# A normed attention stage in a four-block image transformer: the turning of Q and K two passes behind the projection

## What is computed

```python
h = _L0_tok_ref(x, ...)
h = h + _L0_attn_ref(_layernorm(h), ...)
h = h + _L0_ffn_ref(_layernorm(h), ...)
h = h + _L1_attn_ref(_layernorm(h), ...)
h = h + _L1_ffn_ref(_layernorm(h), ...)     # the stage l1f
h = h + _L2_attn_ref(_layernorm(h), ...)
...
```

## Time and profile before

| | |
|---|---|
| median of three runs | 762.44 us (762.32 to 763.35) |
| profiled execution | 763.16 us, its span 761.4 us |
| PE, matmul | 708.0 us busy, 93% of the span |
| PE, weight load | 626.6 us, 82% |
| DVE | 494.7 us, 65% |
| ACT | 345.8 us, 45% |
| POOL | 164.4 us, 22% |
| chain that ended last | PE 68%, DVE 20%, issue 4%, POOL 3%, ACT 3%, DMA 1% |
| mean granted clock of TensorE | 0.946 of full speed |

### The profile page before, as it was taken

One profiled execution on the slowest core, in us unless ns is written; L12 is line 12 of the kernel. 1 busy time (PEld: TensorE's weight loads), 2 busy tenths in 40 slices (PEclk: granted clock), 3 DMA queues, 4 the chain that ended last, 5 costly groups with the idle time before them and its releaser, 6 DMA issues.

```text
span 761.4 us, 15938 instructions
## 1 busy us (share of the span) xinstructions
PE 708.0 (93%) x6222; PEld 626.6 (82%) x6222; DVE 494.7 (65%) x1231; ACT 345.8 (45%) x800; POOL 164.4 (22%) x164
## 2 busy tenths in 40 slices
PE   7799999999998799899899998999999999999996
PEld 6588898999985666688776787889999867789996
DVE  1748478888777836466553674478666768456784
ACT  0257354555452133576423432355544545247653
POOL 1200036444242021334111000016443220000000
PEclk9899999999999879899799997999999999769998
DMA  9912022223220000000200010032130200112100
GB/s 263 251 55 79 2 56 77 77 77 104 94 64 0 1 0 2 2 2 1 96 1 1 2 43 2 1 100 58 58 114 23 86 1 3 50 38 74 36 22 24
DMA packets 16200, 38.81 MB, mean 51 GB/s; under 512 B 3577, under 2 KB 4569, under 8 KB 15740
## 3 DMA queue, kind: packets, MB, share of 16 engines
q1 hardware_dynamic: 14150, 36.71, 16.6%
q10 hardware_dynamic: 1976, 1.08, 0.6%
HBM read 37.32 MB, written 0.44 MB: 50 GB/s over the span
## 4 chain that ended last, share of the span: by engine, by line
PE 68%; DVE 20%; issue 4%; POOL 3%; ACT 3%; DMA 1%; POOLq 0%; ACTq 0%; DVEq 0%; SPq 0%
PE PS L711 7%; PE PS L767 5%; PE PS L543 4%; PE PS L547 4%; PE PS L545 4%; PE PS L544 4%; PE PS L546 4%; PE PS L659 4%; PE PS L700 3%; PE PS L595 3%; PE PS L732 2%; POOL ssq L1767 2%; DVE AL L1438 2%; PE PS L596 2%; PE PS L597 2%
## 5 line engine op out<-in xcount | busy, mean ns | idle before, releaser
L936 ACT ACTIVATE MIX<-PS 128x288 f32<-128x288 f32 x118 | 48.5, 411 | 114.8 <-PE PS L547 114.6
L543 PE MATMUL PS<-XH,WH 128*128 128x288 f32 x284 | 87.3, 307 | 2.2 <-DVE OT L1427 1.4
L545 PE MATMUL PS<-XH,WL 128*128 128x288 f32 x284 | 84.7, 298 | 0.0
L544 PE MATMUL PS<-XL,WH 128*128 128x288 f32 x284 | 84.7, 298 | 0.0
L546 PE MATMUL PS<-X,WH 128*128 128x288 f32 x284 | 84.6, 298 | 0.0
L547 PE MATMUL PS<-X,WL 128*128 128x288 f32 x284 | 84.5, 298 | 0.0
L1740 POOL TENSOR_TENSOR rstd<-var,nhalf 96x3 f32<-96x3 f32 x18 | 15.3, 849 | 305.5 <-DVE var L1195 305.5
L1427 DVE TENSOR_TENSOR OT<-MIX,PS 128x288 f32<-128x288 f32 x94 | 42.3, 451 | 39.7 <-ACT MIX L936 39.0
L1438 DVE TENSOR_TENSOR AL<-OT,AH 128x288 fp32r<-128x288 f32 x118 | 59.0, 508 | 3.3 <-ACT AH L950 2.3
L1281 DVE TENSOR_TENSOR WL<-RG,WH 128x768 fp32r<-128x768 f32 (+2 forms) x46 | 57.9, 1258 | 4.4 <-ACT WH L916 4.3
L595 PE MATMUL PS<-AH,DW 128*128 128x288 f32 x166 | 52.6, 317 | 7.2 <-DVE AL L1438 7.0
(11 more groups left out here) (234 smaller groups left out, 1687.8 us busy)
## 6 DMA issues: line engine op xcount, KB each, us to landing
RG<-in_gu_l0f_dram SPq DMA_DIRECT2D x8, 512.0 KB, 4.6
RG<-in_gu_l0f_dram SPq DMA_DIRECT2D x16, 256.0 KB, 5.7
RG<-in_gu_l2f_dram SPq DMA_DIRECT2D x9, 384.0 KB, 3.5
RG<-in_gu_l2f_dram SPq DMA_DIRECT2D x18, 192.0 KB, 4.3
RD<-in_wd_l0f_dram SPq DMA_DIRECT2D x8, 384.0 KB, 3.2
RD<-in_wd_l2f_dram SPq DMA_DIRECT2D x9, 288.0 KB, 2.8
RD<-in_wd_l3f_dram SPq DMA_DIRECT2D x6, 384.0 KB, 3.2
BIG<-in_patch_dram SPq DMA_DIRECT2D x6, 288.0 KB, 7.5
```

The lines of the kernel that those rows point to most:

```text
L543: mm(o, WH[r][:, 0, w], XH[:, cols], start=True, stop=False)
L544: mm(o, WH[r][:, 0, w], XL[:, cols], start=False, stop=False)
L545: mm(o, WL[r][:, 0, w], XH[:, cols], start=False, stop=False)
```

## The change

The turning of unit u moves from pass u+1 to pass u+2 (`lag` = 2 for this stage alone), and with it the scores, the softmax, the turned probabilities and the product with V of each unit move one pass later, on PE, ACT and DVE. The loops have 18 passes in place of 17. `first_out` stays at pass 13, since the maximum of line 69 gives 13 for either lag, and so do the three parts of the next layer norm on DVE. `TX` gets a third buffer, and ACT's copy into it waits for the turning of unit u-3 in place of u-2. DVE's product with the power for unit i-1 runs at the head of pass i, ahead of `mean_square(i)`, in place of unit i's behind `shift` in pass i. No instruction is added or removed.

```diff
-        self.lag = 1 if token_major else 0
+        self.lag = 2 if qk_norm else 1 if token_major else 0
+        self.txs = 3 if qk_norm else 2
...
-            TX = [sb1(f"TX{r}", [TP, TAU * 256]) for r in range(2)]
+            TX = [sb1(f"TX{r}", [TP, TAU * 256]) for r in range(3)]
...
-                                          TX[u % 2][:, (2 * tau + k) * a.fq:(2 * tau + k + 1) * a.fq],
+                                          TX[u % a.txs][:, (2 * tau + k) * a.fq:(2 * tau + k + 1) * a.fq],
...
-                    act.wait_ge(S["qk_ready"], u0 + u - 1)
-                    activation(TX[u % 2][:, :], PSF[0:TP, 1024:1024 + TAU * 256], ACT.Copy).then_inc(S["tm_taken"], 1)
-
-                lag = 1 if a.tm else 0
+                    act.wait_ge(S["qk_ready"], u0 + u - 2)
+                    activation(TX[u % a.txs][:, :], PSF[0:TP, 1024:1024 + TAU * 256], ACT.Copy).then_inc(S["tm_taken"], 1)
+
+                lag = a.lag
...
-                    tx = TX[u % 2][:, 0:TAU * 2 * a.fq].rearrange("p (h d) -> p h d", d=64)
+                    tx = TX[u % a.txs][:, 0:TAU * 2 * a.fq].rearrange("p (h d) -> p h d", d=64)
...
-                lag = 1 if a.tm else 0
+                lag = a.lag
                 for i in range(a.units + lag + 4):
+                    if a.qk_norm and 1 <= i <= a.units:
+                        normalised_heads(i - 1)
                     if a.qk_norm and i < a.units:
                         mean_square(i)
...
                         shift(i - lag - 1)
-                    if a.qk_norm and i < a.units:
-                        normalised_heads(i)
```

More of the change, by code:

```diff
@@ L680, in qk @@
                                     last = mm(PS[VW * r:VW * (r + 1), k, tau * TP // 2:(tau + 1) * TP // 2].rearrange("f (i m) -> f i m", m=NB),
-                                              TX[u % 2][:, o:o + VW],
+                                              TX[u % a.txs][:, o:o + VW],
                                               cst[0:TP, 0:TP].rearrange("p (i r m) -> p r i m", r=2, m=NB)[:, r],
@@ L1252, in rotate @@
                 link(V.tensor_tensor(t2[:, 1:f2:2], src[:, 0:f2:2], si[:, 1:f2:2], ALU.mult))
-                V.tensor_tensor(TX[u % 2][:, 0:2 * TAU * VW].rearrange("p (n x) -> p n x", x=VW)[:, :, 0:a.fq],
+                V.tensor_tensor(TX[u % a.txs][:, 0:2 * TAU * VW].rearrange("p (n x) -> p n x", x=VW)[:, :, 0:a.fq],
                                 T2[:, f2:2 * f2].rearrange("p (n x) -> p n x", x=a.fq),
```

## The result

Before and after were run in turn on one chip: 762.58 us before (762.32 to 763.35, four runs), 752.76 us after (752.39, 752.75, 752.78 and 764.68). The ratio is 0.9868, with a 95% interval from 0.9849 to 0.9887. The forecast was 756.6 us and the range 752.0 to 761.3.

What follows compares the result with a forecast made beforehand. PE, busy 93% of the span, was taken as the bound, its passes paced by a 5.68 us DVE and POOL loop. Gains 2.4 + 3.1 + 0.3 = 5.8 us took 762.44 to 756.6 us; range 752 to 761.3.

Steps and rivals of the forecast that it cites:

- start, to the projection of pass 6: Stage start: lost time falls from 6.6 to 4.0 us, with a new 2.0 us wait for ACT's copy; 2.4 us taken.
- middle, to the end of pass 11: Passes 6 to 11: DVE's loop with POOL opens, passes fall from 5.68 to PE's 5.15 us; 3.1 us gained.
- end, to `l2a`: Stage end: lost time falls from 7.8 to 7.5 us, with new waits for `norm` of 1.5 and 2.5 us; 0.3 gained.
- the walk: Start gain counted by walking the times to the projection of pass 5, with 1.9 us of work moved behind: 2.2 us.
- The rival without half clock: No half clock after the new waits at start and end: 1.6 + 2.5 us more gain, 752.5 us; chance 0.14.
- passes over 5.2 us: Sign of being wrong: passes 6 to 11 longer than 5.2 us, where 5.15 was forecast.
- The rival of unchanged passes: Middle passes stay at 5.68 us, as the power stretches or something replaces the product: 759.7 us; chance 0.12.
- The step that `norm` would wait for the power's end: Middle: `norm`'s products wait for POOL's power, as a 1.22 us DVE operation took 1.83 beside POOL; loop 4.9 us, not 4.3.
- the rival of half clock through the stage's end: Half clock from pass 13 to the stage's end: 12.8 us more, 769.4 us; chance 0.06.
- one longer stretch: One 13.3 us half-clock stretch at the end costs 6.6 us, not 2.5: 760.7 us; chance 0.10, shared with no net effect.
- half clock already under the 36 records: Sign of being wrong: granted clock of 0.50 already during the 36 matmul records of the output projection, L767.
- Later stages keep their work: Behind the changed stage: later stages keep their work and their loads, which start earlier; no gain counted there.

Runs made afterwards that it cites:

- a3: The changed kernel as it is, run again on the third chip: 754.2 us, ratio 0.9890 to the kernel before.
- a2: The changed kernel as it is, run again on the second chip: 764.7 us, ratio 1.0017 to the kernel before.
- e1: The changed kernel with the product back behind `shift` in its own pass, so lag and third buffer only: 767.0 us, ratio 1.0044.
- e7: The changed kernel with the first half's output one pass later and six unread 288-column matmuls in each of passes 12 and 13: 753.0 us, ratio 0.9896.
- e8: The changed kernel, output where it was, with six unread 288-column matmuls in each of passes 12 and 13: 756.8 us, ratio 0.9928.
- e9: e7 with 14 more unread matmuls in pass 3, ahead of the projection that waits for ACT: 752.6 us, ratio 0.9899.
- b1: The kernel before with unread 288-column matmuls added, 24 in pass 2, 22 in pass 12, 6 in pass 13: 756.5 us, ratio 0.9904.
- e4: The changed kernel with the first half's output and the next layer norm's DVE parts one pass later: 753.9 us, ratio 0.9868.
- p3: The changed kernel with 22 unread 288-column matmuls between the changed stage and the next: 761.1 us, ratio 0.9983.

## Why the prediction was right, point by point

The total lay in the range, 3.8 us below the forecast, and the mechanism of the middle is the one forecast; that the total lay there is in part luck (below). The stage is cut here at the projection of pass 6 and at the end of pass 11, and the 2.5 us of work that the lag moves from the start to the end are set off. The gains on before, for all three profiles of the changed kernel:

| gain, us | forecast | after | a3 | a2 |
|---|---|---|---|---|
| start, to the projection of pass 6 | 2.4 | 2.1 | 0.6 | -1.6 |
| middle, to the end of pass 11 | 3.1 | 2.8 | 2.8 | 2.8 |
| end, to `l2a` | 0.3 | 1.3 | -3.3 | -5.5 |
| stage | 5.8 | 6.3 | 0.1 | -4.2 |

Only the middle came in every profile. The points that follow are of the first one, after.

**Start.** From the first projection to that of pass 6: 59.1 us before, 54.5 after; less 2.5 of moved work, a gain of 2.1 (forecast 2.4, or 2.2 by the walk). Each of its details came: the product at 302.17 behind `gates`, the transposes of unit 0 waiting 0.59 us (forecast 0.35), then

```profile
304.99 0.80 ACT L1097 ACTIVATE TX<-PS 96x768 f32<-96x768 f32 x1
...
305.84 4.57 PE L660 MATMUL PS<-wqkv_l1f,XT 128*96 128x256 f32 x12 [1.95 <-ACT TX L1097]
```

the wait for ACT's copy, and half clock over the projection behind it, 4.57 us as against the 4.63 of the earlier trace rows. The rival without half clock fell here, and again at 377.68.

**Middle.** From the projection of pass 6 to the end of pass 11: 34.1 us before, 31.3 after: 2.8 us for the forecast's 3.1. The pass is PE's own work, 5.20 us and not the 5.15 read from pass 5. That stands at the edge of the sign given for being wrong, "passes over 5.2 us" (they are 5.18 to 5.21 apart), but no other engine stands in the chain, so the 0.05 us is the size of PE's work. The rival of unchanged passes fell; e1 shows what it would have looked like.

**The shared ports.** The step that `norm` would wait for the power's end didn't come. In the fence of pass 8 above, L1620 and L1625, which both read SBUF twice, start 1.39 and 1.59 us into the 2.26 us power and end before it, in 0.16 and 0.46 us. In e1 the same two start at 357.02 and 357.22, between two powers, and take 0.16 and 0.46 us. The power took 2.26 to 2.27 us with `norm` beside it and without. So the reading of the earlier trace rows was carried to a pair to which it doesn't apply. The exclusive lock of the Trainium skill, SBUF — State Buffer, section "SBUF: two separate sides", which I had set beside it, isn't seen here: the trace disagrees for this pair. The loop from one sum of squares to the end of the product was 4.5 us by that (the product starts 0.03 us after the power ends, and DVE is idle for 0.72 of the pass's 5.21 us ahead of the next sum of squares) and not 4.9. Nothing in the sum hung on it.

**End.** From the end of pass 11 to `l2a`: 26.1 us before, 27.3 after, 2.5 of it moved work: a gain of 1.3 us for a forecast of 0.3. Of the difference 0.5 was a slip: the loss of before was counted from the end of pass 11, and pass 11's own 0.5 us, which had no part in it, was taken off again. The rest are sizes. Passes 12 and 13 lost 0.77 us and not 1.0, and for another cause, a wait that the forecast put at nothing: with no projection in front, pass 12's transposes come before ACT has taken the queries of unit 9 out of PSUM; the product of unit 11 and `shift(9)` were in time. And PE came to `l2a` 15.2 us after the 36 records, not 15.5.

**The clock in passes 12 and 13.** This is the step that failed, though not in the runs first timed. I counted passes 12 and 13 at full speed, with 1.0 us of waits, and gave the rival of half clock through the stage's end 0.06, and one longer stretch 0.10, because each wait was shorter than before. In two of the three profiled executions of the changed kernel half clock began there, with one wait of 0.77 us and small matmuls only, and in e1 it began behind none over 0.3 us. So waits shorter than those of before were no ground for full clock. That the first executions kept full clock there was luck: the sign given for being wrong, half clock already under the 36 records, came in a2 and a3. In the profiles with the fill, e7, e8 and e9, it never did. How the small difference at pass 3 becomes a longer half clock there and another in pass 12 is only read from profiles; no run varied it by itself, and it stays open.

**What was not in the prediction at all** is the 4.1 us behind the stage. "Later stages keep their work" was right and not enough: they don't keep their clock. Without them the profiled execution would have been 763.16 - 6.6 = 756.5 us, 0.9 below the 757.4 forecast for it; so the total of 752.8 is no evidence for the sum. The stage's 6.3 us are, for that execution; over three profiles only the middle's 2.8 is.

## What to carry to other kernels

A short wait that recurs in every pass, with another engine's idle time in the same place of its order, is a loop: look for the one step whose result nobody needs until the next pass, and move it past the wait, with the consumer's lag moved along, since neither alone was faster here (0.997 and 1.004). Where a stage has passes without dense work, look at what the clock does there, in more than one execution: here the changed kernel gained 1.3%, nothing and 1.1% on three chips. Six unread matmuls a pass went with full clock up to the output projection in all three profiles that had them and, with the output one pass later, with a stage of 109 to 110 us in place of 113 to 124; with the output where it was (e8), the median time was no better for them, and the same kind of fill in the kernel before gave 1% with no change of order at all (b1). And judge a change of one stage by that stage's own length in the trace, since the same later stages took anything from 364 to 371 us with the same work.

## What the runs showed of the hardware

The later stages' 3,060 or so matmul records, unchanged, took between 341.2 (b1) and 348.4 us (before) of PE's busy time, with a granted clock of 0.97 to 0.94 over the stretch. Over 77 to 80 us of them, with the same waits, the clock was 0.83 in before and 0.89 in after.

Half clock began in a pass with a single wait of 0.77 us (a2, a3, e4) and in one behind none over 0.3 us (e1), and then held into the 36 matmuls of 192 columns behind (7.7 to 8.9 us in place of 6.14). It didn't begin there in the three profiles in which six matmuls of 288 columns (1.06 us) stood in each of passes 12 and 13, nor in two of the six without them. The same pass 0, with no difference in its instructions, took 19.5 us (e8), 20.4 (nine kernels, with the stage's first projection at 270.7 to 272.1) or 22.9 to 23.2 (a2, e9, p3, b1: at 272.6 to 274.6).

A small power on GpSimd (96x12, 2.26 us) and VectorE's products of two SBUF operands ran side by side with neither any longer, while for the pair of the earlier trace rows, a 0.96 us operation of GpSimd and VectorE's of 1,024 columns, the latter took 1.83 us in place of 1.22.
